# Two edits to the order of work in a graph network kernel: the end of the degree count, and the first step's attribute sum

## The reference, cut to what matters

```python
h = relu(layernorm(x))
H = h @ W.T + b;  H = (H - mean(H)) * rsqrt(var(H) + eps) * gamma + beta     # over the nodes
deg = 1 + segment_sum(ones, dst);  dinv = rsqrt(deg)
out = segment_sum(H[src] * dinv[src] * dinv[dst], dst) + H * dinv ** 2
x = x + relu(out)
h = relu(layernorm(x))
agg = segment_sum(edge_attr, dst)                                            # 206,250 x 128
m = concat([h, agg, u[0]])
x = x + relu(relu(m @ W1 + b1) @ W2 + b2) @ W3 + b3
```

## Time and profile before

| | us |
|---|---|
| median of 3 timed runs | 729.8 (727.41 to 731.34) |
| the profiled execution's own time | 722.88 |
| its span, first to last instruction | 721.1 |
| TensorE, matmuls: busy in the span | 665.7 (92%) |
| VectorE busy | 567.3 (79%) |
| ScalarE busy | 457.2 (63%) |
| mean granted clock of TensorE, as a share of full speed | 0.976 |

### The profile page before, as it was taken

How to read it: one execution, slowest core, us unless ns; L and a number is a source line. 1 busy time by engine, 2 the same in 40 slices (tenths; PEclk the granted TensorE clock), 3 DMA queues, 4 the chain that set the end, 5 groups by cost and what they waited for, 6 DMA issues and landing times. The chain is left out here.

```text
span 721.1 us, 21554 instructions
## 1 busy us (share of the span) xinstructions
PE 665.7 (92%) x9010; PEld 571.8 (79%) x9010; DVE 567.3 (79%) x1106; ACT 457.2 (63%) x811; POOL 153.0 (21%) x205
## 2 busy tenths in 40 slices
PE   3986657999999999999999999989999999998997
PEld 2765555888888889888888889978988888896554
DVE  7997988988888888888888886688888889835632
ACT  4563685666667666666666766376666676667863
POOL 8752832110111111110011111010000000013622
PEclk9997697999999999999999999999999999999999
DMA  9002514645455655544444556555444456660122
GB/s 256 19 1 86 194 25 172 228 171 178 175 184 215 218 218 218 215 172 174 171 175 187 216 218 219 207 217 207 176 173 173 178 210 218 218 175 5 43 60 77
DMA packets 64972, 119.75 MB, mean 166 GB/s; under 512 B 3170, under 2 KB 22832, under 8 KB 64900
## 3 DMA queue, kind: packets, MB, share of 16 engines
q1 hardware_dynamic: 63332, 117.82, 46.5%
q0 software_dynamic: 576, 1.12, 0.6%
q10 hardware_dynamic: 1008, 0.07, 0.1%
HBM read 115.81 MB, written 4.03 MB: 166 GB/s over the span
## 5 line engine op out<-in xcount | busy, mean ns | idle before, releaser
L1608 PE MATMUL ps_product<-counts_sb,table_sb 128*128 128x240 f16 (+1 forms) x2646 | 408.4, 261 | 0.0
L1442 ACT CAST counts_sb<-ps_counts 128x588 f16<-128x588 f32 x524 | 336.1, 649 | 100.0 <-PE ps_counts L1598 56.6
L1598 PE MATMUL ps_counts<-key_hot,lo_hot 128*128 128x147 bf16 x2096 | 384.6, 231 | 13.0 <-ACT counts_sb L1442 4.5
L1608 PEld LDWEIGHTS ps_product<-counts_sb,table_sb 128*128 128x128 f16 x2646 | 240.2, 97 | 8.2
L1598 PEld LDWEIGHTS ps_counts<-key_hot,lo_hot 128*128 128x128 bf16 x2096 | 198.1, 98 | 57.8 <-ACT counts_sb L1442 17.9
L902 DVE TENSOR_TENSOR key_hot<-key,iota_key 128x1176 bf16<-128x1176 f16 x262 | 200.8, 766 | 0.0
L898 DVE TENSOR_TENSOR lo_hot<-src_lo,iota_key 128x1024 bf16<-128x1024 f16 x262 | 181.1, 691 | 17.0 <-PE ps_counts L1598 12.6
L1426 POOL TENSOR_SCALAR place_hot<-iota_c,slot_now 128x96 f32<-128x96 f32 x81 | 62.1, 779 | 461.6 <-PE ps_place L1644 452.2
L908 DVE TENSOR_TENSOR attr_hot<-rel,iota_w 128x640 f32<-128x640 int16 x81 | 66.7, 826 | 55.4 <-PE ps_sums L1618 55.4
L1618 PE MATMUL ps_sums<-attr,attr_hot 128*32 128x128 f32 x3240 | 95.5, 276 | 0.0
L1618 PEld LDWEIGHTS ps_sums<-attr,attr_hot 128*32 128x32 f32 x3240 | 88.1, 111 | 4.5 <-issue 4.1
(11 more groups left out here) (295 smaller groups left out, 537.1 us busy)
## 6 DMA issues: line engine op xcount, KB each, us to landing
attr<-in_edge_attr_dram SPq DMA_DIRECT2D x80, 1280.0 KB, 8.2
acc<-in_x_dram SPq DMA_DIRECT2D x4, 768.0 KB, 9.5
attr<-in_x_dram SPq DMA_DIRECT2D x12, 256.0 KB, 5.1
out_dram<-y_ring SPq DMA_DIRECT2D x12, 256.0 KB, 2.3
src_padded<-in_src_dram SPq DMA_DIRECT2D x1, 805.5 KB
attr<-in_edge_attr_dram SPq DMA_DIRECT2D x2, 320.0 KB, 7.8
attr<-in_edge_attr_dram SPq DMA_DIRECT2D x1, 640.0 KB, 3.8
raw_d<-in_dst_dram SPq DMA_DIRECT2D x1, 480.0 KB
```

Source lines behind the costliest of these rows:

```text
L1442: act.copy(counts_sb[s % 2][:].rearrange("p h (n t) -> p h n t", n=WN) [:, :, :, k * QUAD:(k + 1) * QUAD], ps_counts[n % 2][:, :, 0:KEYS]. ...
L1598: ins = pe.matmul(ps_counts[quad % 2][:, c, 0:KEYS], lo_hot[:, held, pair, :, q % 2], key_hot[:, held, pair, :, q % 2], start=True, stop=True)
L1608: ins = pe.matmul(ps_product[side][:, 0:SLOTS] if tiles == TS else product, table_sb[:, h, low, :], counts_sb[side][:, h, :] if tiles == T ...
```

## The change

In stage 1 the placements move from turns 9, 11 and 12 to 9, 12 and 13, so the second kind follows the last turning and `apply_linear(11)`, and the third kind follows `apply_linear(12)`. VectorE normalizes chunk 12 right after chunk 10, and does `begin_pass` before the last three statistics.

In step 0 of stage 3 the 60 products of the attribute sum no longer come in one piece. `sum_attr_spread(q)` gives one or two of them behind the build of each tile from 12 to 51: 60 x (q - 12) // 40 to 60 x (q - 11) // 40, in the same order of kind, `t` and `g`. It waits for the attributes and hots of a kind before its first product. The attribute hots of step 0 are made before batch 2 instead of after it. The save of the sums stands before quad 13 instead of quad 6, the placing at tile 72 instead of 40, the addition in step 1 after its batch 1, and the attribute hots of step 1 after batch 9 instead of batch 5.

```diff
-            DEGREES_AT = {9: 0, 11: 1, 12: 2}
+            DEGREES_AT = {9: 0, 12: 1, 13: 2}
...
                     normalize(10)
+                    normalize(12)
                     link(make_blocks(v, 1))
...
-                    normalize(12)
-                    for c in range(5, 8):
+                    for c in range(5, CHUNKS - 3):
                         bn_part(c)
-                    for c in range(8, CHUNKS):
+                    begin_pass(v, link)
+                    for c in range(CHUNKS - 3, CHUNKS):
                         ins = bn_part(c)
                     link(ins)
                     v.bn_aggr(bn[:, 0:2], bstats[:].rearrange("p c k -> p (c k)")).then_inc(bn_ok, 1)
-                    begin_pass(v, link)
...
+        SPREAD, SPREAD_END = 12, 52
...
-                                sum_at = SHORT_SUM_AT if s == SHORT else LATE_SUM_AT if s > SHORT else SUM_AT
+                                sum_at = (SHORT_SUM_AT if s == SHORT else SPREAD_END if s == 0 else
+                                          LATE_SUM_AT if s > SHORT else SUM_AT)
...
-                                sum_at, place_at = ((LATE_SUM_AT, LATE_PLACE_AT) if s > SHORT else (SUM_AT, PLACE_AT))
+                                sum_at, place_at = ((LATE_SUM_AT, LATE_PLACE_AT) if s > SHORT or s == 0 else
+                                                    (SUM_AT, PLACE_AT))
+                                if s == 0:
+                                    make_attr_hots(0)
                                 for b in range(FIRST_OCTS if s == 0 else 0, OCTS):
                                     make_oct(s, b)
-                                    if s == 0 and b == FIRST_OCTS:
-                                        make_attr_hots(0)
...
-                                    if s < SHORT and b == place_at // OCT + 3:
+                                    if 0 < s < SHORT and b == place_at // OCT + 3:
                                         add(s)
-                                    if s > LATE and b == 1:
+                                    if (s > LATE or s == 1) and b == 1:
                                         add(s - 1)
...
+                            def sum_attr_spread(q):
+                                parts, tiles = R * GT * CG, SPREAD_END - SPREAD
+                                for part in range(parts * (q - SPREAD) // tiles, parts * (q - SPREAD + 1) // tiles):
+                                    j, rest = divmod(part, GT * CG)
+                                    t, g = divmod(rest, CG)
+                                    if rest == 0:
+                                        pe.wait_ge(attr_hots, j + 1)
+                                        pe.wait_ge(attr_in[j], 16)
+                                    ins = pe.matmul(ps_sums[g * W:(g + 1) * W, j * P:(j + 1) * P],
+                                                    attr_hot[:, j, t, g, :],
+                                                    attr[:, j * CG + g, t * P:(t + 1) * P],
+                                                    start=(t == 0), stop=(t == GT - 1))
+                                    if rest == GT * CG - 1:
+                                        ins.then_inc(summed, 1)
...
-                                sum_at, place_at = (LATE_SUM_AT, LATE_PLACE_AT) if like >= 5 else (SUM_AT, PLACE_AT)
+                                sum_at, place_at = (LATE_SUM_AT, LATE_PLACE_AT) if like >= 5 or first else (SUM_AT, PLACE_AT)
...
-                                    if q == sum_at:
+                                    if first and SPREAD <= q < SPREAD_END:
+                                        sum_attr_spread(q)
+                                    elif q == sum_at and not first:
                                         sum_attr(s)
```

More of the change, by code:

```diff
@@ L1651, in step @@
                                 octs = s * OCTS - (OCTS - SPARES // OCT if like >= 5 else 0)
-                                sum_at, place_at = (LATE_SUM_AT, LATE_PLACE_AT) if like >= 5 else (SUM_AT, PLACE_AT)
+                                sum_at, place_at = (LATE_SUM_AT, LATE_PLACE_AT) if like >= 5 or first else (SUM_AT, PLACE_AT)
                                 for q in range(TS):
-                                    if q == sum_at - 1:
+                                    if q == sum_at - 1 and not first:
                                         pe.wait_ge(attr_hots, s * R + R)
@@ L1658, in step @@
                                         pe.wait_ge(taken, s - 2)
-                                    ready_to_sum(s, first, sum_at - q)
+                                    if not first:
+                                        ready_to_sum(s, first, sum_at - q)
                                     ready_to_place(s, first, place_at - q)
```

## The result

| | kernel before | changed kernel |
|---|---|---|
| median of 4 timed runs, us | 728.71 (727.41 to 731.34) | 748.91 (746.57 to 750.36) |
| the profiled execution's own time, us | 722.88 | 750.36 |
| its span, us | 721.1 | 748.5 |
| mean granted clock | 0.976 | 0.951 |

The ratio is 1.0265, with a 95% interval from 1.0227 to 1.0302: the change makes the kernel 16.5 to 22 us slower. The forecast was 737.4 with a range from 730 to 747: the sign was right, the forecast's +7.6 less than half of what came, and 748.9 lies outside the range.

A forecast was written before the change was run, and what follows sets the result against it. It took TensorE's instruction stream to bound most of the span. Step 0 +8.5 us and stage 1 -0.9 us gave +7.6, from the timed median of 729.8 to 737.4 us, range 730 to 747.

The forecast's parts named there:

- The sum: Stage 3, step 0: tiles 12 to 51 priced at 0.73 us until 117.4, then 0.49; step 0 ends 8.5 us later.
- first rival: Step 0: the clock doesn't rise, 38 tiles at 0.73 us; +16.0, with stage 1 +15.1, 744.9 us; chance 0.21.
- Turns and passages: Step 0: unshared column-group turns and pauses at 80 shape changes make a tile with its visit 0.49 us at 2.4 GHz.
- The lower clock's price: Step 0: at 1.2 GHz a tile with its visit costs 0.73 us: 0.21 in, 0.22 turn, 0.30 out.
- Cover: Step 0: everything but TensorE is off the path; VectorE is ahead, attribute reloads arrive in time with 3 us slack.
- Passages free: Step 0: pauses vanish in short visits, turns remain; 0.28 us per tile, +1.4, 730.3 us in all; chance 0.11.
- faster: Step 0, tiles 14 to 79: TensorE has room, ScalarE sets the pace; -5.4, with stage 1 -6.3, 723.5 us; chance 0.09.
- Stage 1: End of stage 1: reordering starts the aggregation at 62.36 and ends the sum into `dinv` earlier; gain 0.9 us, bounds 0 and 1.1.
- The base: Whole kernel: +7.6 us on the profiled 722.88 gives 730.5; timed median 729.8, 6.9 higher, gives 737.4.

The follow-up runs named there:

- warm: Step 0 edit on the kernel before, plus 44 full-width matmuls nobody reads between tile 11 and the first visit; 745.4 us in one run.
- three or five bursts: Step 0 edit on the kernel before, but the 60 products in three bursts of 20 (0.9991, 730.2 us) or five of 12 (1.0002, 731.3 us).
- fours: Step 0 edit on the kernel before, but the 60 products in 15 visits of four, one per column group; ratio 1.0023, 731.9 us.
- filler: Step 0 edit on the kernel before, plus one full-width matmul nobody reads behind every build of tiles 12 to 51; ratio 1.0181, 744.2 us.
- full width: Step 0 edit on the kernel before, same 40 visits, but each product on all 128 columns instead of 32; 734.7 us in one run.
- only step 0: The changed kernel without the stage 1 edit, against the kernel before; ratio 1.0270, 752.2 us.
- one burst: Step 0 edit on the kernel before, but all 60 products in one burst behind tile 24; ratio 0.9992, 730.9 us.

## Why the prediction was wrong, point by point

The failing step is in *The sum*: "Up to 117.4, 4.95 / 0.73 = 6.8 tiles. The other 31.2 tiles take 31.2 x 0.49". The clock's rise at 117.4 was taken from the kernel before as if it belonged to the place, but the change removes the burst inside which it stood. In its place the runs showed a granted clock of 0.5 from the first visit to the end of the spread (rise at 152.7), and all 40 visits at the lower clock's 0.805 us. With the clock up from the first visit ("warm") step 0 would be some 7.3 us longer than before, close to the +8.5 of the sum; the other 12.8 of the 20.0 are the clock. That the burst lifts it is read from this: with one, three or five bursts or with fours the clock rose 1.4 to 6.7 us after the first of them began, each time during narrow products of all four groups or at most 1.3 us after them. No run leaves them out without putting something else in their place, so the builds, which also came further apart between the visits, may have a part in it. The text had this case as its first rival, saw the reason ("what lifted it was the burst", "three of four column groups unused") and gave it 0.21, up to 747, because TensorE would be "never without an instruction from 112.45 on". The filler and the warm start show that this argument was worth nothing: marked busy 4.00 of 4 us, with the clock up and with it down.

- *Turns and passages.* Right, as a mechanism and at the upper clock as a size: 0.49 predicted, 0.51 measured once the clock was made to be up. Two turns of 0.11 and a build of 0.06 are 0.28 of it; of the other 0.23 the passages' own share is 0.18, by "full width". "Fours" and "full width" show the two parts one by one: turns shared by four groups, and passages that vanish with the shape.
- *The lower clock's price.* 0.73 predicted, 0.805 measured (40 visits in 32.2 us). I took the way out as 0.20 with its turn doubled, 0.30; it was 0.36 (121.23 less the second half's start, 0.21 after 120.66). Over 38 tiles that is 2.8 us of the 4.0 by which the rival's +16.0 falls short of the measured +20.0 in step 0. The remaining 1.2 lie behind the spread, where 16 more tiles were built at the lower clock; the text let step 0 end at the old pace there. That the rival's 744.9 is also 4.0 below 748.9 is chance: it was counted from 729.8 where the kernel before has 728.7, and with 0.9 gained in stage 1.
- *Cover.* Right: VectorE waited for TensorE up to 5 us at a time, no reload of attributes was late, and step 1 and what follows took as long as before (592.1 and 592.3 us from its first product to the end; 593.9 in "only step 0", where the clock was still low as step 1 began).
- *"Passages free" and "faster".* Refuted: 0.18 us per visit for its two passages, and in no kernel with visits of one or two parts did a tile with its visit take under 0.33.
- *Stage 1.* Gain of 0.9 predicted, bound 1.1; 1.4 measured inside the stage, nothing that can be measured in the whole. The aggregation started at 62.51, as predicted (62.36), but the last placement came after it. I had VectorE late at the end; in the traces it waits 1.0 to 1.3 us for the last placement where TensorE came late. That term didn't matter for the outcome.
- *The base.* The profiled execution of before was the only one of thirteen with a stage 2 of 41 us. The sum was made against it and then moved to the median, which kept this out of the forecast; comparing the two profiled executions directly would have given 27.5 us instead of 20.2.

## What to carry to other kernels

In this kernel narrow products (32 of 128 columns) were cheap only in bunches of all four column groups, and each change between narrow and full-width matmuls cost a pause that the profile puts under "issue" (0.18 us for the two of a visit at the upper clock); deal them out in bunches at points where the next engine has work in hand, not one by one. When a change thins out the stretch in which TensorE's clock rose, price the whole stretch after it at the lower clock as well, and take that as the forecast unless a row shows the same mix lifting it. A work-around for a wait is placed by the buffers of the engine that waits: the same five bursts gained nothing two tiles into a quad and, moved to quad ends with the hots back in their place, they went with a gain of 0.7%.

## What the runs showed of the hardware that was not expected

- The mark of busy says nothing on the clock: 20.00 of 20 us busy at 0.50 for the spread in the changed kernel, and the same mix at 1.00 throughout when it began there. The Trainium skill ("TensorE: Matmul & The Clock Gate", Part 1: The HAM clock gate) says that the clock follows how busy the array has been; this case agrees only if busy is not read from the profile's mark.
- Adding a matmul of 0.11 to 0.21 us to each of 40 tiles shortened step 0 from 41.8 to 36.9 us.
- Builds at ScalarE's pace alone didn't hold the clock in every run: in "one burst" it fell again after the burst (0.63 in 132 to 136, 0.52 in 136 to 140; the columns are TensorE's busy us and count, clock, DMA share and GB/s), and in "fours" from 134.2 to 137.6, where the kernel before kept 1.00 in the same part of the step. Both have a step 0 some 2 us longer than the kernel before.

```profile
132.00:136.00 4.00, 3.14 (x21) 0.63 1.04 397
136.00:140.00 4.00, 3.75 (x26) 0.52 0.09 32
```

- Between executions of almost the same code, pauses of 0.5 to 1.2 us without any wait for data come and go in TensorE's list in stage 2; the one execution in thirteen without them, which also had less of the lower clock there, had a stage 2 shorter by 7 us.
